# TensorE signals its edge products, turned rows and layer results by a drain behind the group

## The chip, the cores and the metric

The kernel runs on one core of a Trainium2 chip. The metric is the time of one execution on the device in microseconds (us), as the median of several runs; lower is better.

## What is computed

A graph network over 3,125 nodes with 256 features and 53,125 edges, sorted by their target. In the reference, cut to its two layers:

```
# layer 0
neighbor = segment_sum(weight[:, None] * x[src], dst)
out = (x @ W1.T + b1) + (neighbor + neighbor * x) @ W2.T + b2
out = where(out >= 0, out, 0.2 * out);  out = out / max(norm(out), 1e-12)
x = layernorm(x + out)
# layer 1: self loops added, whose edge attributes are zero
e = relu(edge_attr @ ee_w1 + ee_b1) @ ee_w2 + ee_b2
agg = segment_sum(x[src] + e, dst)
h = (1 + eps) * x + agg
h = relu(ln(h @ w1 + b1, g1, be1))      # 256 -> 1024
h = relu(ln(h @ w2 + b2, g2, be2))      # 1024 -> 1024
out = relu(ln(x + h @ w3 + b3, bn_g, bn_b))
x = layernorm(x + out)
```

## The kernel before

Nodes are worked in 25 blocks of 128 rows, edges in tiles of 128: 17 tiles per block, 8 in the last, taken in pairs (nine steps per block, the ninth a single tile; four in the last block). The program has two stages, one after the other on every engine, and each has a general version that does not run on this graph.

**The edge stage.** For each tile GpSimd (POOL) gathers 128 rows of x by the edges' sources (L970). TensorE (PE) multiplies the edge attributes by ee_w1 (`edge_layer`, L1108) for a pair of tiles into one of three banks `ps_e` and signals `edge_net`. ScalarE (ACT) and VectorE (DVE) make the message `msg` of the pair out of both, as a high part and a low remainder (L1658 and L1661 on ACT, L2162 and L2168 on DVE), and DVE signals `message`. PE sums a tile's messages per target by a product with a one-hot matrix, once for the high part (L1113) and once for the low part (L1115). The edge product runs three pairs ahead (`LEAD`) of the sums, and waits for the message of the pair two before it. When a block is summed, PE turns its four pieces of 128 columns (`turn`, L1143) and signals `s_turned`; ACT copies the turned rows to `sT`, and three small products (L1183, L1190, L1209), spread over the next blocks, give the layer's rows, which go to HBM as a table.

**The network stage.** POOL gathers rows of that table (L1031), PE sums them per target (`near_step` of the second stage, L1330 and L1335), and the block's h passes through the three layers. Here each product is made of three in `three` (L1386): high by high, high by low, low by high. Per block PE has `turn_h` (two turns of h, signals `h_turned`), `layer1` for each half of the 1,024 columns (6 products of 512 wide each, signals `z_done[0]`), `layer2` for each half (24 products each, signals `z_done[1]`), `layer3` (24 products of 256 wide in two halves, signals `y_done` after the second) and `turn_z` for each of layers 1 and 2 and each half (four turns of `zn`, L1455, signals `turned2`). Between them DVE takes statistics of the layer's rows (L2480), ACT and DVE normalize to `zn` (L1876, L2505), ACT applies scale, shift and relu to the turned rows (L1888), and DVE splits the result into high and low parts (L2523, L2525), which PE's next layer waits for.

The order on PE is written out by hand. `iteration`, which a loop runs for 21 blocks (L1584), interleaves neighbouring blocks: layer 2 of block i - 1 (first half), `turn_h` of i, the second half of layer 2, three sum tiles of i + 1, layer 1 of i, `turn_z` of layer 2 of i - 1 (both halves), further sum tiles, `turn_z` of layer 1 of i, and layer 3 of i - 1 around its second half. Each wait is either attached to the instruction behind it or stands as a semaphore instruction of PE's sequencer ahead of it.

In all these groups the last matmul carries the signal, by `mm.then_inc(...)`.

Of the kernel before, what the change touches and what calls it, by code (L numbers as in the profile page):

```python
# [31 lines left out]
N, E, D, ED, H = 3125, 53125, 256, 64, 1024  # L32
P = 128
# [22 lines left out]
KD = D // 128  # L56
KH = H // 128
# [6 lines left out]
def wait(eng, sem, value):  # L64

    if isinstance(value, int) and value <= 0:
        return
    eng.wait_ge(sem, value)
# [168 lines left out]
def exists(b):  # L237

    return not isinstance(b, int) or 0 <= b < BLOCKS
# [32 lines left out]
def gnn_program(nc, x, xT, src, dst, weight, attrT, w1T, w2T, bias01, bias02, eps_in, ee_w1, ee_b1row, ee_b1,  # L272
# [6 lines left out]
    with ExitStack() as keep:  # L279
        def sb(name, shape, dt, ctx=keep):  # L280
            return ctx.enter_context(nc.sbuf_tensor(name, shape, dt))

        def psum(name, shape, ctx):
            return ctx.enter_context(nc.psum_tensor(name, shape, F32))
# [10 lines left out]
        ident = sb("ident", [P, P], F32)  # L295
# [13 lines left out]
        with ExitStack() as ca:  # L309
            def sa(name, shape, dt):  # L310
                return sb(name, shape, dt, ca)

            def ma(name):
                return sem(name)
# [8 lines left out]
            attr = sa("attr", [ED + 1, TILES * P], F32)  # L323
# [28 lines left out]
            we1 = sa("we1", [ED + 1, D], F32)  # L352
# [13 lines left out]
            s_r = sa("s_r", [P, 2 * D], F32)  # L366
# [15 lines left out]
            ps_e = [psum(f"ps_e{n}", [P, 512], ca) for n in range(3)]  # L382
            ps_t = psum("ps_t", [128, 512], ca)
# [20 lines left out]
            edge_net = ma("edge_net")  # L404
# [6 lines left out]
            s_turned = ma("s_turned")  # L411
# [104 lines left out]
        with ExitStack() as cb:  # L516
            def s2(name, shape, dt):
                return sb(name, shape, dt, cb)

            def m2(name):  # L520
                return sem(name)
# [9 lines left out]
            w1_low = s2("w1_low", [128, KD, H], F32R)  # L531
            w2_low = s2("w2_low", [128, KH, H], F32R)
            w3_low = s2("w3_low", [128, KH, D], F32R)
            w1_high = s2("w1_high", [128, KD, H], F32R)
# [5 lines left out]
            h = s2("h", [P, D], F32)  # L540
            ident_r = s2("ident_r", [P, P], F32R)
            place(msg_base)
            w2_high = s2("w2_high", [128, KH, H], F32R)
            place(msg_base + 8 * 16 * D)
            grow = s2("grow", [P, TILES, 2 * D], F32R)
            hT = s2("hT", [128, 2, KD * P], F32R)
# [13 lines left out]
            w3_high = s2("w3_high", [128, KH, D], F32R)  # L560
# [4 lines left out]
            zn = s2("zn", [P, H], F32)  # L565
# [4 lines left out]
            ps_z = [psum(f"ps_z{n}", [P, 2, 512], cb) for n in range(2)]  # L570
            ps_tr = psum("ps_tr", [128, 2, 512], cb)
            ps_y = psum("ps_y", [P, 512], cb)
# [19 lines left out]
            h_turned = m2("h_turned")  # L592
            hT_high, hT_ready = m2("hT_high"), m2("hT_ready")
            z_done = [m2(f"z_done{n}") for n in range(2)]
# [4 lines left out]
            turned2 = [m2(f"turned2_{n}") for n in range(2)]  # L599
            relu_out = [m2(f"relu_out{n}") for n in range(2)]  # L600
            a_ready = [m2(f"a_ready{n}") for n in range(2)]
            y_done = m2("y_done")
# [56 lines left out]
            def a_of(layer, p):  # L659

                if isinstance(p, int) and (layer, p) in ((0, LAST), (1, LAST - 1)):
                    return (a2, a1)[layer]
                return (a1, a2)[layer]

            def z_of(layer, p):

                return ps_z[0] if layer == 1 and isinstance(p, int) and p == LAST else ps_z[layer]
# [424 lines left out]
        def _(pe):  # L1092
# [9 lines left out]
            def edge_layer(q, k, start=0):  # L1102

                j0, m = PAIRS[k]
                pe.wait_ge(attr_in[k // 3], 16 * (q + 1 + (1 if start else 0)))
                wait(pe, message, start + NP * q + k - 2)
                for j in range(j0, j0 + m):
                    mm = pe.matmul(ps_e[k % 3][:, (j - j0) * D:(j - j0 + 1) * D],  # L1108
                                   attr[:, j * P:(j + 1) * P], we1[:, :], start=True, stop=True)
                mm.then_inc(edge_net, 1)  # L1110

            def add_tile(bank, j, slot, start, stop):
                pe.matmul(ps_sum[bank][:, :], oh[:, slot, :], msg[:, j, 0, :], start=start, stop=False,  # L1113
# [24 lines left out]
            def turn(b):  # L1138

                pe.wait_ge(s_ready, b + 1)  # L1140
                wait(pe, sT_ready, b)
                for n in range(4):
                    mm = pe.transpose(ps_t[:, n * P:(n + 1) * P], s_r[:, n * 128:(n + 1) * 128], ident[:, :])  # L1143
                mm.then_inc(s_turned, 1)

            def count(acc, first, end, n, chain):

# [143 lines left out]
            def second_stage():  # L1291
# [83 lines left out]
                def turn_h(path, b):  # L1375
                    pe.wait_ge(h_ready, b + 1)

                    wait(pe, relu_out[0 if path.skewed else 1], 2 * b)
                    for k in range(KD):
                        mm = pe.transpose(ps_tr[:, 0, k * P:(k + 1) * P], h[:, k * 128:(k + 1) * 128], ident[:, :])  # L1380
                    mm.then_inc(h_turned, 1)

                def three(acc, left, right, stop):

                    for a, b in ((0, 0), (0, 1), (1, 0)):
                        mm = pe.matmul(acc, left[a], right[b], start=False, stop=stop and a == 1,  # L1386
                                       skip_group_check=True)
                    return mm

                def layer1(b, n):  # L1390
                    if n == 0:
                        pe.wait_ge(hT_ready, b + 1)
                    pe.wait_ge(z_open[0][n], b + 1)
                    cols = slice(n * 512, (n + 1) * 512)
                    for k in range(KD):
                        mm = three(ps_z[0][:, n, :], [hT[:, a, k * P:(k + 1) * P] for a in range(2)],
                                   [w[:, k, cols] for w in (w1_high, w1_low)], k == KD - 1)
                    mm.then_inc(z_done[0], 1)

                def layer2(b, n, first=0, end=KH):  # L1400
                    if first == 0:
                        pe.wait_ge(z_open[1][n], b + 1)
                    cols = slice(n * 512, (n + 1) * 512)
                    for k in range(first, end):
                        if n == 0 and k % 4 == 0:
                            pe.wait_ge(a_ready[0], 2 * b + k // 4 + 1)
                        mm = three(z_of(1, b)[:, n, :], [a_of(0, b)[:, a, k, :] for a in range(2)],
                                   [w[:, k, cols] for w in (w2_high, w2_low)], k == KH - 1)
                    if end == KH:
                        mm.then_inc(z_done[1], 1)  # L1410

                def layer2_with(b, n, w, first, end):

# [17 lines left out]
                def layer3(b, half):  # L1431
                    if half == 0:
                        pe.wait_ge(y_open, b + 1)
                    pe.wait_ge(a_ready[1], 2 * b + half + 1)
                    for k in range(half * KH // 2, (half + 1) * KH // 2):
                        mm = three(ps_y[:, 0:D], [a_of(1, b)[:, a, k, :] for a in range(2)],
                                   [w[:, k, :] for w in (w3_high, w3_low)], k == KH - 1)
                    if half == 1:
                        mm.then_inc(y_done, 1)

                def turn_z(path, layer, b, half, free=None):

                    if free:
                        pe.wait_ge(relu_out[free[0]], 2 * free[1] + half + 1)
                    elif layer == 0:
                        pe.wait_ge(hT_ready, b + 1)
                        wait(pe, relu_out[1], 2 * (b - 1) + half + 1)
                    else:
                        pe.wait_ge(relu_out[0], 2 * b + half + 1)
                        if path.skewed and exists(b + 1):  # L1450
                            pe.wait_ge(hT_ready, b + 2)
                    pe.wait_ge(zn_ready[layer][half], b + 1)
                    for c in range(4):
                        k = 4 * half + c
                        mm = pe.transpose(ps_tr[:, half, c * P:(c + 1) * P], zn[:, k * 128:(k + 1) * 128],  # L1455
                                          ident[:, :])
                    mm.then_inc(turned2[layer], 1)

                def is_late(i):

# [7 lines left out]
                def first_block(path):  # L1468
# [6 lines left out]
                    pe.wait_ge(dd_end[-1], DD)  # L1475
                    copy_highs(2, 4)
                    turn_h(path, 0)
                    copy_highs(4, 6)
                    pe.wait_ge(w_ready, LAYER_1 - 1)
                    layer1(0, 0)  # L1480
                    copy_highs(6, 7)
                    pe.wait_ge(w_ready, LAYER_1)
                    layer1(0, 1)
                    copy_highs(7, 9)
                    for c in path.ahead[0:2]:
                        near_step(path, 1, c)
                    turn_z(path, 0, 0, 0)
                    pe.wait_ge(w_ready, 6)
                    turn_z(path, 0, 0, 1)
                    copy_highs(9, 11)  # L1490
                    for c in path.ahead[2:]:
# [1335 lines left out]
```

## Time and profile before

| | before |
|---|---|
| time, median of 3 runs | 1,134.37 us (1,134.0 to 1,136.73) |
| span of the profiled execution | 1,477.5 us |
| PE matmul busy | 1,201.4 us (81%), 5,297 matmuls |
| DVE busy | 976.8 us (66%) |
| POOL busy | 812.9 us (55%) |
| ACT busy | 686.1 us (46%) |
| mean granted TensorE clock | 0.891 of full speed |

The profiled execution is 343 us longer than the timed median. Its durations of single instructions can be read as they are; its idle stretches can't be carried over to a timed run as they are. The profile records the start of every matmul and models its end, so that rows of neighbouring matmuls overlap. "PEld" is the load of the weights that a matmul uses, and an engine's name with a q behind it is its sequencer, which works through waits, register work and drains.

### The profile page before, as it was taken

The numbers are of one execution on the slowest core, as the hardware profiler recorded it, in microseconds if no ns is written. First come the engines' busy times: TensorE is split into PE (matmuls) and PEld (weight loads), VectorE is DVE, ScalarE is ACT, GpSimd is POOL, SyncE is SP. The second block draws the span as 40 slices with busy tenths as digits, with TensorE's granted clock in tenths as the row PEclk, the third lists the DMA queues.
The fourth block names the chain that finished last, engine by engine and source line by source line (L and its number), as shares of the span: only waits on it lengthen the run. The fifth ranks groups of instructions, "written<-read, shape, count | busy, mean of one in ns | idle before, by whom it ended". The sixth has DMA issues, their size and how long they took to land.

```text
span 1477.5 us, 21215 instructions
## 1 busy us (share of the span) xinstructions
PE 1201.4 (81%) x5297; PEld 977.9 (66%) x5297; DVE 976.8 (66%) x2795; ACT 686.1 (46%) x1677; POOL 812.9 (55%) x840
## 2 busy tenths in 40 slices
PE   4788877787777887778777889888898898898897
PEld 3576666566666665566555677677776777776676
DVE  4767755667656775667666666666666676676575
ACT  2455644556445554455453443443533443443444
POOL 7555555455554555545645565566565566566530
PEclk9798887888878888788878899999999999999999
DMA  6345544445444444435565555656665566566540
GB/s 202 105 120 145 151 130 144 125 142 147 134 143 128 128 127 119 126 114 148 146 203 163 165 169 172 185 167 183 176 185 166 174 176 178 171 185 180 161 119 13
DMA packets 106088, 222.13 MB, mean 150 GB/s; under 512 B 20003, under 2 KB 57369, under 8 KB 106010
## 3 DMA queue, kind: packets, MB, share of 16 engines
q0 software_dynamic: 53408, 164.16, 39.1%
q1 hardware_dynamic: 52602, 57.11, 12.4%
q8 instruction: 27, 0.44, 0.1%
q14 instruction: 51, 0.42, 0.1%
HBM read 203.96 MB, written 17.23 MB: 150 GB/s over the span
## 4 chain that ended last, share of the span: by engine, by line
PE 34%; another core or an unknown queue 21%; DVE 16%; issue 16%; ACT 11%; DVEq 1%; DMA 1%; POOL 1%; ACTq 0%; POOLq 0%
PE ps_z L1386 8%; PE ps_e L1108 7%; PE ps_sum L1115 3%; PE ps_sum L1113 3%; ACT msg L1658 3%; ACT aF L1888 3%; PE ps_y L1386 3%; PE ps_s L1330 3%; DVE msg L2162 2%; DVE oh L216 2%; PE ps_tr L1455 2%; DVE msg L2168 2%; PE ps_w L1209 2%; ACT msg L1661 2%
## 5 line engine op out<-in xcount | busy, mean ns | idle before, releaser
L970 POOL DMA_INDIRECT raw<-in_x,src_all x399 | 385.6, 966 | 321.9 <-DVE msg L2168 177.2
L1031 POOL DMA_INDIRECT grow<-table_dram,src_all x401 | 392.7, 979 | 275.0 <-issue 115.1
L1108 PE MATMUL ps_e<-we,attr 65*128 65x256 f32 x832 | 251.1, 427 | 150.7 <-DVE msg L2168 127.0
L2162 DVE SCALAR_TENSOR_TENSOR msg<-raw,w_sb,msg 128x256 fp32r<-128x256 f32 x416 | 183.0, 478 | 242.5 <-issue 130.5
L1108 PEld LDWEIGHTS ps_e<-we,attr 65*128 65x128 f32 x832 | 171.5, 214 | 200.4 <-issue 173.3
L1661 ACT ACTIVATE msg<-ps_e 128x512 fp32r<-128x512 f32 (+1 forms) x220 | 124.3, 565 | 310.2 <-remote 221.1
L1113 PE MATMUL ps_sum<-msg,oh 128*128 128x512 f32 x464 | 255.8, 551 | 9.2 <-DVE msg L2168 8.8
L1386 PE MATMUL ps_z<-w_high,a 128*128 128x512 f32 x784 | 255.5, 395 | 7.7 <-issue 6.3
L216 DVE TENSOR_SCALAR oh<-lane,rel 128x128 fp32r<-128x128 f32 x871 | 208.1, 297 | 18.9 <-issue 15.7
L1115 PE MATMUL ps_sum<-msg,oh 128*128 128x512 f32 x464 | 210.1, 453 | 0.0
L1658 ACT ACTIVATE msg<-raw,w_sb 128x256 fp32r<-128x256 f32 x416 | 188.1, 498 | 10.3 <-issue 7.7
L1386 PEld LDWEIGHTS ps_z<-w_high,a 128*128 128x128 f32 x784 | 147.0, 188 | 40.1 <-issue 9.5
L1888 ACT ACTIVATE aF<-ps_tr,be,g 128x128 f32<-128x128 f32 x392 | 147.3, 464 | 53.7 <-PE ps_tr L1455 33.1
L1386 PE MATMUL ps_z<-w_low,a 128*128 128x512 f32 x392 | 153.4, 391 | 1.0 <-issue 0.8
L2168 DVE SCALAR_TENSOR_TENSOR msg<-ps_e,msg 128x512 fp32r<-128x512 f32 (+1 forms) x220 | 143.6, 653 | 0.0
L1455 PE MATMUL ps_tr<-ident,zn 128*128 128x128 f32 x400 | 64.3, 301 | 76.5 <-issue 38.8
L1113 PEld LDWEIGHTS ps_sum<-msg,oh 128*128 128x128 f32 x464 | 102.9, 222 | 34.0 <-issue 11.7
L1115 PEld LDWEIGHTS ps_sum<-msg,oh 128*128 128x128 f32 x464 | 104.1, 224 | 22.4
L1455 PEld LDWEIGHTS ps_tr<-ident,zn 128*128 128x128 f32 x400 | 50.1, 155 | 89.0 <-issue 88.4
L1330 PE MATMUL ps_s<-grow,oh 128*128 128x512 f32 x365 | 104.2, 429 | 0.4 <-issue 0.4
L1386 PE MATMUL ps_y<-w_high,a 128*128 128x256 f32 x400 | 89.6, 306 | 4.1 <-DVE a L2538 2.1
L1386 PEld LDWEIGHTS ps_z<-w_low,a 128*128 128x128 f32 x392 | 73.8, 188 | 18.6 <-issue 5.2
(189 smaller groups left out, 1591.6 us busy)
## 6 DMA issues: line engine op xcount, KB each, us to landing
attr<-in_attrT SPq DMA_DIRECT2D x50, 192.0 KB
raw<-in_x,src_all POOLq DMA_INDIRECT x416
grow<-table_dram,src_all POOLq DMA_INDIRECT x401
w_raw<-in_m_w SPq DMA_DIRECT2D x48, 128.0 KB
table_dram<-table SPq DMA_DIRECT2D x23, 256.0 KB
attr<-in_attrT SPq DMA_DIRECT2D x24, 160.0 KB
xs<-in_x SPq DMA_DIRECT2D x24, 128.0 KB
xTb<-in_xT SPq DMA_DIRECT2D x24, 128.0 KB
```

The lines of the kernel that those rows point to most:

```text
L216: ins = dve.tensor_scalar(out_[:, i, :], lanes, which[:, i:i + 1], None, ALU.is_equal)
L970: pool.indirect_dma_start(out=raw[:, j, :], out_offset=None, in_=x, in_offset=bass.IndirectOffsetOnAxis(ap=src_all[:, q * TILES + j:q * TI ...
L1031: pool.indirect_dma_start(out=grow[:, j, :].bitcast(F32), out_offset=None, in_=table_dram, in_offset=bass.IndirectOffsetOnAxis(ap=src_all[ ...
L1108: mm = pe.matmul(ps_e[k % 3][:, (j - j0) * D:(j - j0 + 1) * D], attr[:, j * P:(j + 1) * P], we1[:, :], start=True, stop=True)
L1113: pe.matmul(ps_sum[bank][:, :], oh[:, slot, :], msg[:, j, 0, :], start=start, stop=False, skip_group_check=True)
L1115: return pe.matmul(ps_sum[bank][:, :], oh[:, slot, :], msg[:, j, 1, :], start=False, stop=stop, skip_group_check=True)
L1386: mm = pe.matmul(acc, left[a], right[b], start=False, stop=stop and a == 1, skip_group_check=True)
L1658: act.activation(msg[:, j, 0, 0:D], raw[:, j, :], ACT.Copy, scale=w_sb[:, tile_cols(n, j)])
L1661: act.activation(msg[:, j0:j0 + m, 0, D:2 * D], ps_e[k % 3][:, 0:m * D].rearrange("p (j d) -> p j d", d=D), ACT.Relu).then_inc(high, 1)
L1888: ins = act.activation(aF[layer][:, k, :], ps_tr[:, half, c * P:(c + 1) * P], ACT.Relu, bias=bb[:, k:k + 1], scale=gg[:, k:k + 1])
L2162: dve.scalar_tensor_tensor(msg[:, j, 1, 0:D], raw[:, j, :], w_sb[:, tile_cols(n, j)], msg[:, j, 0, 0:D].bitcast(F32), ALU.mult, ALU.subtract)
L2168: dve.scalar_tensor_tensor(msg[:, j0:j0 + m, 1, D:2 * D], ps_e[k % 3][:, 0:m * D].rearrange("p (j d) -> p j d", d=D), 0.0, msg[:, j0:j0 + ...
```

## The change

On PE, in `edge_layer`, `turn`, `turn_h`, `layer1`, `layer2`, `layer3` and `turn_z`, the signal is taken off the group's last matmul. Behind the group stands a drain, and that carries the signal. The semaphores, their values and all who wait for them stay as they are, and so does the order of all other instructions on every engine. The signals of the sum tiles (`summed`, `sum_done`), of the small products (`dense`, `edge_dense`), of layer 2 of block 0 (which has its own code, `layer2_with`) and of layer 3 of the last block stay on matmuls.

```diff
@@ edge_layer
-                    mm = pe.matmul(ps_e[k % 3][:, (j - j0) * D:(j - j0 + 1) * D],
-                                   attr[:, j * P:(j + 1) * P], we1[:, :], start=True, stop=True)
-                mm.then_inc(edge_net, 1)
+                    pe.matmul(ps_e[k % 3][:, (j - j0) * D:(j - j0 + 1) * D],
+                              attr[:, j * P:(j + 1) * P], we1[:, :], start=True, stop=True)
+                pe.drain().then_inc(edge_net, 1)
@@ turn
-                mm.then_inc(s_turned, 1)
+                pe.drain().then_inc(s_turned, 1)
@@ turn_h
-                    mm.then_inc(h_turned, 1)
+                    pe.drain().then_inc(h_turned, 1)
@@ layer1
-                    mm.then_inc(z_done[0], 1)
+                    pe.drain().then_inc(z_done[0], 1)
@@ layer2
                     if end == KH:
-                        mm.then_inc(z_done[1], 1)
+                        pe.drain().then_inc(z_done[1], 1)
@@ layer3
                     if half == 1:
-                        mm.then_inc(y_done, 1)
+                        pe.drain().then_inc(y_done, 1)
@@ turn_z
-                    mm.then_inc(turned2[layer], 1)
+                    pe.drain().then_inc(turned2[layer], 1)
```

## Rows read from the trace of the kernel before

**Rows 1.** Windows: length, busy of PE, PEld, DVE, ACT, POOL; clock, DMA share, GB/s:

```profile
0.00:25.30 25.30, 14.11 (x36) 10.30 (x37) 13.94 (x40) 7.81 (x16) 18.12 (x23) 1.00 0.84 248
25.30:731.50 706.20, 553.19 (x2133) 443.23 (x2132) 467.16 (x1367) 367.05 (x890) 384.62 (x398) 0.83 0.46 132
...
731.50:769.60 38.10, 26.41 (x110) 20.07 (x109) 22.64 (x64) 18.29 (x44) 17.57 (x19) 0.80 0.60 178
...
769.60:1424.10 654.50, 565.27 (x2785) 468.27 (x2785) 439.31 (x1244) 266.95 (x665) 391.70 (x400) 0.95 0.60 175
```

**Rows 2.** Who waited on PE for whom: total us, times, longest; edge, then network stage:

```profile
PE ps_e L1108 <- DVE msg L2168: 127.0, 37, 7.6
...
PE ps_tr L1455 <- issue: 38.8, 21, 4.5
PE ps_tr L1455 <- ACT zn L1876: 35.0, 16, 6.0
```

**Rows 3.** Grouped instructions: count | busy us, mean ns | idle before us:

```profile
L1386 PE MATMUL ps_z<-w_high,a 128*128 128x512 f32 x784 | 255.5, 395 | 7.7 <-issue 6.3 <-DVE a L2525 1.2
L1108 PE MATMUL ps_e<-we,attr 65*128 65x256 f32 x832 | 251.1, 427 | 150.7 <-DVE msg L2168 127.0 <-issue 18.8 <-remote 4.9
```

**Rows 4.** Timeline of an edge group and its sum tiles: start us, us, matmuls, then loads:

```profile
606.10 1.03 PE L1108 MATMUL ps_e<-we,attr 65*128 65x256 f32 x4
606.78 0.59 PE L1113 MATMUL ps_sum<-msg,oh 128*128 128x512 f32 x1
...
606.75 0.19 PEld L1113 LDWEIGHTS ps_sum<-msg,oh 128*128 128x128 f32 x1
```

**Rows 5.** Timeline of PE at turn_z and layer 3, network stage:

```profile
1126.08 0.60 PE L1455 MATMUL ps_tr<-ident,zn 128*128 128x128 f32 x4
...
1127.47 0.40 PE L1386 MATMUL ps_y<-w_high,a 128*128 128x256 f32 x2
...
1127.83 0.28 PE L1386 MATMUL ps_y<-w_high,a 128*128 128x256 f32 x1
...
1126.40 0.19 PEld L1386 LDWEIGHTS ps_y<-w_high,a 128*128 128x128 f32 x1
```

**Rows 6.** Timeline behind layer 2, then the wait of L1393 (last: its time):

```profile
1110.19 0.39 PE L1386 MATMUL ps_z<-w_high,a 128*128 128x512 f32 x1
1110.42 0.84 PE L1330 MATMUL ps_s<-grow,oh 128*128 128x512 f32 x3
...
1111.52 0.40 PE L1386 MATMUL ps_z<-w_low,hT 128*128 128x512 f32 x1
...
1110.19 0.64 PEld L1330 LDWEIGHTS ps_s<-grow,oh 128*128 128x128 f32 x3
1111.18 0.19 PEld L1386 LDWEIGHTS ps_z<-w_high,hT 128*128 128x128 f32 x1 [0.34 <-DVE hT L2475]
...
L1393 PEldq EVENT_SEMAPHORE  x1: 51/51/51, 1110.1 to 1110.1; - x1
```

**Rows 7.** Timeline at the end: the last product and who takes it:

```profile
1469.90 0.28 PE L1386 MATMUL ps_y<-w_high,a 128*128 128x256 f32 x1
1470.22 0.42 DVE L2556 TENSOR_TENSOR t<-ps_y,hbx 128x256 f32<-128x256 f32 x1 [0.40 <-PE ps_y L1386]
```

**Rows 8.** PE's sequencer: duration ns min/median/max, first and last start us:

```profile
L279 PEldq DRAIN  x1: 68/68/68, 1472.6 to 1472.6; - x1
...
L1126 PEldq EVENT_SEMAPHORE  x23: 51/51/51, 81.7 to 734.1; - x23
...
L1584 PEldq COMPARE_BRANCH  x21: 76/208/228, 850.4 to 1404.2; - x21
```

**Rows 9.** Timeline of POOL, one gather (one of a row of such):

```profile
613.31 0.95 POOL L970 DMA_INDIRECT raw<-in_x,src_all  x1 [0.30 <-issue]
```

**Rows 10.** Chain of work, start us, us, what; then the window around it as Rows 1:

```profile
631.22 0.43 PE ps_sum L1113
...
631.00:633.00 2.00, 2.00 (x6) 1.61 (x5) 1.70 (x7) 2.00 (x6) 0.70 (x1) 0.50 0.58 168
```

More of the change, by code:

```diff
@@ L1142, in turn @@
                 for n in range(4):
-                    mm = pe.transpose(ps_t[:, n * P:(n + 1) * P], s_r[:, n * 128:(n + 1) * 128], ident[:, :])
-                mm.then_inc(s_turned, 1)
+                    pe.transpose(ps_t[:, n * P:(n + 1) * P], s_r[:, n * 128:(n + 1) * 128], ident[:, :])
+                pe.drain().then_inc(s_turned, 1)
             def count(acc, first, end, n, chain):
@@ L1379, in turn_h @@
                     for k in range(KD):
-                        mm = pe.transpose(ps_tr[:, 0, k * P:(k + 1) * P], h[:, k * 128:(k + 1) * 128], ident[:, :])
-                    mm.then_inc(h_turned, 1)
+                        pe.transpose(ps_tr[:, 0, k * P:(k + 1) * P], h[:, k * 128:(k + 1) * 128], ident[:, :])
+                    pe.drain().then_inc(h_turned, 1)
                 def three(acc, left, right, stop):
@@ L1395, in layer1 @@
                     for k in range(KD):
-                        mm = three(ps_z[0][:, n, :], [hT[:, a, k * P:(k + 1) * P] for a in range(2)],
-                                   [w[:, k, cols] for w in (w1_high, w1_low)], k == KD - 1)
-                    mm.then_inc(z_done[0], 1)
+                        three(ps_z[0][:, n, :], [hT[:, a, k * P:(k + 1) * P] for a in range(2)],
+                              [w[:, k, cols] for w in (w1_high, w1_low)], k == KD - 1)
+                    pe.drain().then_inc(z_done[0], 1)
                 def layer2(b, n, first=0, end=KH):
@@ L1406, in layer2 @@
                             pe.wait_ge(a_ready[0], 2 * b + k // 4 + 1)
-                        mm = three(z_of(1, b)[:, n, :], [a_of(0, b)[:, a, k, :] for a in range(2)],
-                                   [w[:, k, cols] for w in (w2_high, w2_low)], k == KH - 1)
+                        three(z_of(1, b)[:, n, :], [a_of(0, b)[:, a, k, :] for a in range(2)],
+                              [w[:, k, cols] for w in (w2_high, w2_low)], k == KH - 1)
                     if end == KH:
-                        mm.then_inc(z_done[1], 1)
+                        pe.drain().then_inc(z_done[1], 1)
                 def layer2_with(b, n, w, first, end):
@@ L1435, in layer3 @@
                     for k in range(half * KH // 2, (half + 1) * KH // 2):
-                        mm = three(ps_y[:, 0:D], [a_of(1, b)[:, a, k, :] for a in range(2)],
-                                   [w[:, k, :] for w in (w3_high, w3_low)], k == KH - 1)
+                        three(ps_y[:, 0:D], [a_of(1, b)[:, a, k, :] for a in range(2)],
+                              [w[:, k, :] for w in (w3_high, w3_low)], k == KH - 1)
                     if half == 1:
-                        mm.then_inc(y_done, 1)
+                        pe.drain().then_inc(y_done, 1)
                 def turn_z(path, layer, b, half, free=None):
@@ L1454, in turn_z @@
                         k = 4 * half + c
-                        mm = pe.transpose(ps_tr[:, half, c * P:(c + 1) * P], zn[:, k * 128:(k + 1) * 128],
-                                          ident[:, :])
-                    mm.then_inc(turned2[layer], 1)
+                        pe.transpose(ps_tr[:, half, c * P:(c + 1) * P], zn[:, k * 128:(k + 1) * 128],
+                                     ident[:, :])
+                    pe.drain().then_inc(turned2[layer], 1)
                 def is_late(i):
```

## Prediction

> **What bounds the kernel now.** I read four views in this order: the busy time of two long windows, the list of who waited for whom on TensorE, the grouped instructions, and then single instructions of two short stretches.
>
> The windows [rows 1] split the span into an edge stage (25.3 to 731.5 us) and a network stage (769.6 to 1424.1 us). TensorE (PE) is the busiest engine in both, 553 of 706 us and 565 of 655 us. Its waits [rows 2] are few in kind (the rows are the long ones). In the edge stage it waits 127 us for messages, all of it ahead of an edge product (L1108) and in only 37 places. In the network stage nearly the whole wait, 38.8 + 35.0 us, is ahead of the turn of a normalized layer (L1455), some 3 us in each of 24 blocks. Everywhere else PE runs one matmul into the next.
>
> How tight is that stream? Busy time overstates it, since each matmul row overlaps the next one. What counts is the distance from start to start. A 512-wide product follows the last after 0.225 us (three in 0.84, the last 0.39 long), a 256-wide one of the last layer after 0.12, a turn (128 wide) after 0.11, four in 0.60 [rows 5, 6]; an edge matmul after 0.217, four in 1.03, the last 0.38 long [rows 4]. With counts from the list of groups (two of some forty in [rows 3]): 1,476 of layers 1 and 2, 928 of the edge stage's sums and 365 of the network stage's, 2,769 x 0.225 = 623; 600 of layer 3 x 0.12 = 72; 832 of the edge product x 0.217 = 181; 400 turns of z x 0.11 = 44; the other 696 of all 5,297, mostly 128 and 256 wide, at an estimated 0.17 each, 118. That makes 1,038 us at the full clock, some 476 of them in the edge stage (181 + 209 and 86 of the others) and 562 in the network stage.
>
> The profiled execution took 1,477.5 us, the timed median is 1,134. That is less than PE's own 1,201 us of busy time in the profile, so the timed run cannot hold the idle stretches that the profile shows: it has 1,134 - 1,038 = 96 us of PE time that is not stream. Some 28 of these no change of this kind can use (11 idle in the first 25 and some 10 of the 12 at the change of stages, 38 us long with 26 busy [rows 1]; 7 from the last product, 1470.18 [rows 7], to the span's end). **So a timed run has at most 68 us of slack on PE, the profiled one over 200 in its waits alone.** This decides more than anything else below.
>
> **The change part by part.** Nothing is moved and no wait is added; on the path that runs, 493 groups lose the signal on their last matmul and get a drain behind it that signals. They are 220 edge groups (24 blocks of 9 pairs, the last of 4), 25 turns of sums, 25 of h, 50 of layer 1, 49 of layer 2 (the first of block 0 has its own code, untouched), 24 of layer 3 (the last block has its own), 100 turns of z.
>
> What goes: the signals on matmuls. They cost nothing today. In [rows 6] the last matmul of a layer-2 group, which signals, starts at 1110.19 and the next group at 1110.42, the same distance as inside a group.
>
> What comes: the drain is an instruction of PE's sequencer, and nothing behind it is handed to the array until it is through. Today the sequencer runs ahead: the wait of L1393 for layer 1 is done at 1110.1, when PE still has a product of layer 2 and three sum tiles to start [rows 6]. And the weight load of the next group starts with the last matmul of this one. That overlap is what a drain takes away. Three cases:
> - Edge group. Its four matmuls end at 607.13, and the weight load of the sum tile starts at 606.75 [rows 4]. With a drain the load starts after 607.13 + 0.068 (the only TensorE drain in the trace, on an idle engine) + 0.051 (the wait that follows it) [rows 8] + some 0.03 to start, at 607.28. Shift 0.53 us, x 220 = 117 us.
> - A 512-wide group: last matmul 1110.19 to 1110.58, next load today at 1110.19, with a drain at 1110.73. After a stop the next pair comes closer: load 1111.18, second matmul 1111.52, 0.34 apart, against two steps of 0.225 in the stream [rows 6]. Shift 0.54 - 0.11 = 0.43.
> - A turn: four end at 1126.68, next load today at 1126.40; with a drain 1126.83, shift 0.43 [rows 5]. Layer 3: its last matmul runs 0.28 from 1127.83 [rows 5], and the next load starts with it; 0.43 again. So (25 + 248) x 0.43 = 117 us.
> - Behind layer 3 comes the loop's end (a branch of 0.208 [rows 8] and three shorter instructions at some 0.04, 0.32 us), hidden today under products in the queue, exposed behind a drain: 21 x 0.32 = 7 us.
>
> Sum: 117 + 117 + 7 = **241 us of PE time**. Lower bound of the price: the tail of a matmul past its successor's start, 0.39 - 0.23 = 0.16, plus drain and wait 0.12, 0.28 each, 138 us in all. Upper bound: each drain is followed not by one but by two sequencer instructions, or by register work in the loop, and costs 0.13 more (0.051 of work and the pause behind it), 305 us. I take 241, since it is built from the very places.
>
> What signals lose: today a consumer starts 0.04 us after the modelled end of a product (1469.90 + 0.28, next the tensor_tensor of L2556 at 1470.22 [rows 7]). With a drain it starts about 0.1 later. On the other engines this adds some 0.1 to each link of the chain products, statistics, normalize, turn.
>
> What hides it. In the network stage the three drains between the end of layer 2 and the turn that waits for it (layer 2 itself, layer 1 twice, 1.3 us) fall into that wait of 3 us, 24 x 1.3 = 31 us, if the timed run has it. In the edge stage GpSimd starts a gather each 0.95 + 0.30 us [rows 9], so 416 of them take at least 520 us, and PE has 520 - 476 = 44 us free; that leaves some 24 of the 68 for the network stage. A stream with breaks in it never fills all of that: I count 20 in each stage as used. **1,134 + 241 - 40 = 1,335 us.**
>
> Against the profiled execution the same sum gives less, since it holds more idle time: the edge stage's 128 us half hidden in its 152 us of waits, +64; the network stage 113 - 31, +82; so 1,477.5 + 146, near 1,625.
>
> A rule on the other side of the row: the Trainium skill, "VectorE: DVE Perf Modes", section "The DRAIN you can't avoid", tells of boilerplate drains of a constant 12 ns on all five engines. By it the 493 would be 6 us. The trace disagrees even for an idle PE, 68 ns [rows 8]. "PSUM — Partial Sum Buffer", section "Engine vs sequencer instructions", says that a drain waits for the engine to go fully idle; by that rule the price is the one worked out above, and no row of this trace has a drain behind running products to show it.
>
> **Rivals.**
> (1) *The gathers pace the edge stage, and a drain overlaps more than I think.* With all 44 us used there and the lower price: 245 x 0.28 - 44 = 25, and 248 x 0.28 + 7 - 20 = 56 in the network stage, 1,134 + 81 = 1,215; with 0.43 everywhere it is 1,289. For it: PE waits 127 us for messages in the edge stage [rows 2], and these come from gathers. Against it: nothing shows a weight load that starts ahead of a drain.
> (2) *Dearer.* Upper price, 305 - 40: 1,399. Or the clock: in the edge stage the granted clock averages 0.83 of 2.4 GHz [rows 1], and in a stretch at 0.50, the level of 1.2 GHz, in which PE had gone idle, a 512-wide product takes 0.43 us of the chain [rows 10]. More gaps may cost more of it; a further tenth of the stream at that level would be 1,038 x 0.1 x (0.43 - 0.225) / 0.225 = 95 us, less what vanished long waits give back. 1,370 to 1,430.
> (3) *The other side: no loss.* The drain returns when all is handed to the array, not when it is through, and the sequencer's lead covers it: 493 x (0.068 + 0.051) = 59 us of sequencer time off the path. Then 1,134, within 0.3% of before. It decides if the sequencer's lead behind a group is over 0.12 us, which [rows 6] show it is; but then consumers would read unfinished sums, which a drain is there to prevent. A gain would need signals that come earlier, and there are 0.04 us to win at each at most.
>
> **How the numbers follow.** My forecast (1,290 to 1,370) 0.57; rival 1 (1,215 to 1,289) 0.22; rival 2 0.17; rival 3 0.03; a gain 0.01. The range 1,230 to 1,410 leaves out the foot of rival 1, rival 3 and the top of rival 2, some 0.15 together. About 0.3% is what a measurement can tell from no change: faster 0.01, same 0.03, slower 0.96.
>
> **What the profile after would show.** Each price: the weight load of L1113 behind an edge group starting 0.1 to 0.2 us after that group's last matmul has ended, instead of with it; gaps of this kind, put down to nothing the profile shows, some 490 times; drains with a row each whose time grows with what is in flight. The stream: fewer waits of PE for messages and for zn. Wrong if weight loads still start under a drained group's last matmul (rival 3), if that start comes less than 0.1 us behind it, while PE still has waits for messages (rival 1), or if the clock of either window falls by over 0.05 (rival 2). The forecast falls too if the timed cost per drain, the difference over 493, lies outside 0.3 to 0.5 us.

## The result, and the profile after

| | before | after |
|---|---|---|
| time, median | 1,134.35 us | 1,320.49 us (1,320.31 to 1,335.18) |
| ratio | | 1.1661, 95% interval 1.1606 to 1.1716 |
| span of the profiled execution | 1,477.5 us | 1,318.7 us |
| the same, second profile of before | 1,135.1 us | |
| PE matmul busy (second profile) | 1,081.8 us (95%) | 1,174.4 us (89%) |
| idle of PE, span less busy (same) | 53 us | 144 us |

The change costs 186 us, 16.6%. The kernel before, unchanged and profiled again (first experiment below), has a span of 1,135.1 us, close to its timed median, so all traces of after are compared with that second one. Ratios leave out disturbed executions, which only experiment 8 had: three of its six, at 1,447.42 to 1,457.88 us.

The page of after: the span, the busy time of each engine with its share, the granted TensorE clock in forty slices, and the chain of work that ended last.

```profile
span 1318.7 us, 21708 instructions
...
PE 1174.4 (89%) x5297; PEld 877.7 (67%) x5297; DVE 985.8 (75%) x2795; ACT 691.0 (52%) x1677; POOL 810.7 (61%) x840
...
PEclk9999999999999999999999999999999999999999
...
PEld 50%; issue 27%; PEldq 12%; DVE 7%; DMA 2%; PE 1%; ACT 1%; POOL 0%; POOLq 0%; DVEq 0%; ACTq 0%
```

The same lines of the second profile of before:

```profile
span 1135.1 us, 21215 instructions
...
PE 1081.8 (95%) x5297; PEld 894.6 (79%) x5297; DVE 986.4 (87%) x2795; ACT 688.1 (61%) x1677; POOL 803.3 (71%) x840
...
PE 50%; POOL 21%; issue 17%; DVE 7%; DMA 3%; ACT 1%; POOLq 0%; DVEq 0%; ACTq 0%
```

There are 493 instructions more, the drains, and the same number of matmuls. PE's busy time is 93 us longer all the same, and that is no further work: a matmul's row overlaps the next one's, and where the stream breaks the overlap is gone, so that the union of the rows grows. Busy and idle time together give the 184 us by which the spans differ. The chain is what changed. Before, it ran over matmuls (PE 50%) and over gathers (POOL 21%). After, it runs over weight loads (PEld 50%), over time in which PE waited for nothing that the profile shows (issue 27%) and over the drains (PEldq 12%), and POOL is no longer in it: a weight load that starts late, behind a drain, is what the end waits for.

An edge group in the timeline of after (start us, length us, in brackets the idle time before and its releaser), which answers to [rows 4], and then the drains of L1110 that touch this stretch (count, shortest/median/longest ns, first and last start):

```profile
300.83 1.03 PE L1108 MATMUL ps_e<-we,attr 65*128 65x256 f32 x4
...
301.92 0.60 ACT L1661 ACTIVATE msg<-ps_e 128x512 fp32r<-128x512 f32 x1 [1.52 <-PEq L1110]
302.06 0.19 PEld L1113 LDWEIGHTS ps_sum<-msg,oh 128*128 128x128 f32 x1 [0.60 <-issue]
302.09 0.47 PE L1113 MATMUL ps_sum<-msg,oh 128*128 128x512 f32 x1 [0.23 <-issue]
...
302.40 0.39 PE L1115 MATMUL ps_sum<-msg,oh 128*128 128x512 f32 x1
```

```profile
L1110 PEldq DRAIN  x2: 2335/2338/2342, 299.5 to 302.2; - x2
```

The edge matmuls' modelled end is 301.86. The first drain runs from 299.5 for 2.34 us and ends at about 301.9 (its row gives starts in tenths; by the trace it ends 0.02 us behind the matmuls); ACT, which waits for it, starts at 301.92. The next weight load starts at 302.06, 0.20 behind the matmuls' end, where before the change it started under them. The same place in the second profile of before:

```profile
302.44 1.03 PE L1108 MATMUL ps_e<-we,attr 65*128 65x256 f32 x4
303.12 0.59 PE L1113 MATMUL ps_sum<-msg,oh 128*128 128x512 f32 x1
303.55 0.39 PE L1115 MATMUL ps_sum<-msg,oh 128*128 128x512 f32 x1
```

The last of the four edge matmuls starts 0.65 behind the first. From it to the second matmul behind the group are 303.55 - 303.09 = 0.46 us before and 302.40 - 301.48 = 0.92 after. Read in this way, to the second matmul, which takes in that the next two matmuls stand closer together after a stop, the typical price of each kind of group is:

| group | drains | shift each, us | sum, us |
|---|---|---|---|
| edge product | 220 | 0.467 | 102.7 |
| turn of the sums | 25 | 0.464 | 11.6 |
| turn of h | 25 | 0.343 | 8.6 |
| layer 1 | 50 | 0.347, 0.424 | 19.3 |
| layer 2 | 49 | 0.523, 0.580 | 27.1 |
| turn of z | 100 | 0.343 to 0.565, mean 0.473 | 47.3 |
| layer 3 | 24 | 0.945 at the loop's end (21), 0.43 taken for the other 3 | 21.1 |
| all | 493 | mean 0.48 | 238 |

Behind layer 3 stands the loop's end, and there the stop is the longest:

```profile
912.34 0.28 PE L1386 MATMUL ps_y<-w_high,a 128*128 128x256 f32 x1
913.30 0.49 PE L1386 MATMUL ps_z<-w_high,a 128*128 128x512 f32 x1 [0.69 <-issue]
913.63 0.40 PE L1386 MATMUL ps_z<-w_low,a 128*128 128x512 f32 x1
```

From 912.34 to 913.63 are 1.29 us, against 0.345 in a stream (0.12 + 0.225).

**By stage.** The edge stage ends with the last sum matmul (L1115); its rows before and after (count, shortest/median/longest ns, first and last start us):

```profile
L1115 PE MATMUL ps_sum<-msg,oh x464: 387/395/628, 21.1 to 533.4; 128*128 128x512 f32 x155
```

```profile
L1115 PE MATMUL ps_sum<-msg,oh x464: 387/392/628, 21.9 to 606.5; 128*128 128x512 f32 x155
```

So the edge stage grew by 73.1 us, the network stage by (1,318.7 - 606.5) - (1,135.1 - 533.4) = 110.5. Of the 114.3 us of drains in the first, 41 are hidden; of the 123.4 in the second, 13.

Both traces hold the same 5,297 matmuls in the same order, so the growth can also be added up place by place, from start to start. At the drained places the spacing grew by 112 us in the edge stage and by 118 in the network stage, 230 in all where the table of typical prices has 238. All other spacings shrank, by 39 us and by 8. In the edge stage 30 of those 39 us lie ahead of an edge product or of the first product of a tile's sum, the places where PE had to wait for messages before the change; now it comes late enough not to. In the network stage, then, some 5 of the 13 hidden us are the table's, and 8 are left; two executions that have no drain in this stage differ there by up to 3 us.

The windows of each stage, after and then before (start and end, length; busy of PE, PEld, DVE, ACT, POOL; clock, DMA share, GB/s), which answer to [rows 1]:

```profile
25.00:606.00 581.00, 524.25 (x2182) 380.39 (x2180) 483.49 (x1385) 378.46 (x907) 398.60 (x408) 1.00 0.59 165
635.00:1300.00 665.00, 602.63 (x2919) 463.18 (x2918) 449.90 (x1263) 275.99 (x695) 377.94 (x392) 1.00 0.58 169
```

```profile
25.00:533.00 508.00, 486.86 (x2180) 390.11 (x2179) 482.65 (x1384) 374.67 (x907) 384.63 (x406) 1.00 0.67 187
561.00:1115.00 554.00, 547.69 (x2909) 468.08 (x2908) 449.75 (x1263) 275.84 (x694) 382.51 (x394) 0.99 0.70 204
```

The clock is at its upper level, 2.4 GHz, in all four. PE's idle share went from 4% to 10% in the edge stage and from 1% to 9% in the network stage.

**Who waits now.** On PE the wait for messages of [rows 2] is gone, and time put down to nothing ("issue") stands first (total us, times, longest):

```profile
PE ps_sum L1113 <- issue: 39.1, 167, 0.4
PE ps_z L1386 <- issue: 15.4, 25, 0.7
...
PE ps_tr L1455 <- ACT zn L1876: 0.9, 1, 0.9
PE ps_e L1108 <- DVE msg L2168: 0.9, 3, 0.4
```

The other engines wait for drains:

```profile
ACT msg L1661 <- PEq L1110: 149.0, 134, 2.5
...
ACT aF L1888 <- PEq L1457: 98.7, 69, 2.2
...
POOL raw L970 <- PEq L1144: 62.0, 21, 6.1
```

These last three look like the loss and are not, as the fourth experiment shows: these engines now follow PE.

### The profile page after: what moved, and what is told of

It reads as the page before. It is cut to its first block, busy times and chain, and to the rows that moved or that the text cites. A ratio compares the mean times of both kernels' runs of the same rounds, so it can differ in the third digit from the quotient of the medians.

```text
span 1318.7 us, 21708 instructions
## 1 busy us (share of the span) xinstructions
PE 1174.4 (89%) x5297; PEld 877.7 (67%) x5297; DVE 985.8 (75%) x2795; ACT 691.0 (52%) x1677; POOL 810.7 (61%) x840
## 4 chain that ended last, share of the span: by engine, by line
PEld 50%; issue 27%; PEldq 12%; DVE 7%; DMA 2%; PE 1%; ACT 1%; POOL 0%; POOLq 0%; DVEq 0%; ACTq 0%
PEld ps_z L1386 19%; PEld ps_e L1108 9%; PEld ps_y L1386 5%; PEld ps_sum L1115 5%; PEldq L1110 3%; PEldq L1144 3%; PEld ps_tr L1455 3%; PEld ps_s L1330 3%; PEld ps_sum L1113 3%; DMA raw<-in_x,src_all 2%; DVE msg L2162 2%; DVE oh L216 1%; DVE msg L2168 1%; PEld ps_d L1190 1%; PEld ps_w L1209 1%
## 5 line engine op out<-in xcount | busy, mean ns | idle before, releaser
L1031 POOL DMA_INDIRECT grow<-table_dram,src_all x401 | 386.5, 964 | 257.7 <-issue 112.1
L1113 PE MATMUL ps_sum<-msg,oh 128*128 128x512 f32 x464 | 199.7, 430 | 51.3 <-issue 39.1
L1108 PE MATMUL ps_e<-we,attr 65*128 65x256 f32 x832 | 222.9, 388 | 7.4 <-issue 5.3
L1108 PEld LDWEIGHTS ps_e<-we,attr 65*128 65x128 f32 x832 | 157.8, 193 | 40.3 <-issue 14.6
L1115 PE MATMUL ps_sum<-msg,oh 128*128 128x512 f32 x464 | 183.1, 395 | 0.0
L1113 PEld LDWEIGHTS ps_sum<-msg,oh 128*128 128x128 f32 x464 | 87.3, 188 | 143.0 <-issue 102.4
L2480 DVE BATCH_NORM_STATS2 bs<-ps_z 128x6 f32<-128x512 f32 x100 | 69.6, 698 | 69.7 <-PEq L1410 41.0
L1330 PE MATMUL ps_s<-grow,oh 128*128 128x512 f32 x365 | 96.5, 403 | 15.2 <-issue 15.1
L2523 DVE CAST a<-aF 128x512 fp32r<-128x512 f32 x98 | 42.0, 429 | 71.4 <-ACT aF L1888 71.4
L1115 PEld LDWEIGHTS ps_sum<-msg,oh 128*128 128x128 f32 x464 | 87.9, 189 | 10.6
L1330 PEld LDWEIGHTS ps_s<-grow,oh 128*128 128x128 f32 x365 | 64.8, 188 | 41.6 <-issue 29.6
L1899 ACT ACTIVATE fm<-fm,ln_eps 128x1 f32<-128x1 f32 x50 | 14.7, 295 | 137.1 <-DVE fm L2485 137.1
```

The lines of the kernel that those rows point to most:

```text
L1031: pool.indirect_dma_start(out=grow[:, j, :].bitcast(F32), out_offset=None, in_=table_dram, in_offset=bass.IndirectOffsetOnAxis(ap=src_all[ ...
L1108: pe.matmul(ps_e[k % 3][:, (j - j0) * D:(j - j0 + 1) * D], attr[:, j * P:(j + 1) * P], we1[:, :], start=True, stop=True)
L1115: return pe.matmul(ps_sum[bank][:, :], oh[:, slot, :], msg[:, j, 1, :], start=False, stop=stop, skip_group_check=True)
L1330: return pe.matmul(ps_s[:, :], oh[:, slot, :], grow[:, j, :], start=start, stop=stop, skip_group_check=True)
```

## The experiments

**1. The kernel before, once more.** No edit. The question was whether the long waits of the first profile belong to the kernel.

> The kernel before, unchanged, for a second profiled execution. The change's profile has a span of 1,318.7 us beside a timed median of 1,320.5, at a mean clock of 0.998; the one of before has 1,477.5 beside 1,134, at 0.891. Theory A: the first profile of before was one disturbed execution; a second one has a span within 1% of 1,134 and a clock near 1. Theory B: the program before is slowed by being profiled, whenever it is (its sequencers run ahead and are held by the records); the span is again near 1,478 with 5 to 7 us pauses of ScalarE and VectorE in each block of the edge stage.

Measured: 1,136.94 us (one execution; seven others of the same kernel beside it have a median of 1,135.65), span 1,135.1 us, mean clock 0.993. The waits of PE that answer to [rows 2]:

```profile
PE ps_e L1108 <- DVE msg L2168: 12.8, 22, 3.1
...
PE ps_tr L1455 <- ACT zn L1876: 3.5, 3, 1.4
```

127 us of waiting for messages are 12.8, and the 74 us ahead of the turn of z are 3.5 and 0.7. So the first profile's 343 us are no fixed property of the program, nor of profiling it as such. What disturbed that execution is not known.

**2. The two halves of the change.** One kernel has the drains of the edge products alone (220), the other the remaining 273. Against the change, e1 puts back, at all places but the first, the form of before:

```diff
-                pe.drain().then_inc(s_turned, 1)
+                mm.then_inc(s_turned, 1)
```

and e2 does so in `edge_layer` only:

```diff
-                pe.drain().then_inc(edge_net, 1)
+                mm.then_inc(edge_net, 1)
```

> Drains behind the 220 edge groups alone, all other groups as before. Stream theory: from the second matmul behind the group, the change's trace shows 0.47 us lost at each, 103 us in all; with the 44 us of slack that I estimated for the edge stage, of which 20 used, 1,134 + 103 - 20 = 1,217; with all 44 used 1,193. Rival, late signals: the loss comes from consumers that start later, and the edge signal is the one that ScalarE waits for 134 times; then this part carries most of the 186 us, over 1,280.

> Drains behind the turns and the layers (273 groups), the edge groups as before. Stream theory: the trace of the change shows 134 us lost at these places (0.34 to 0.58 each, 0.94 behind layer 3); 20 hidden, 1,134 + 134 - 20 = 1,248. With the edges-only kernel it adds up to the change, since the stages follow one another: the two losses sum to 186 within 10. Rival, late signals: under 1,200 if the edge signal carries the loss.

Measured: the edges alone 1,196.82 us, ratio 1.0575 (1.0502 to 1.0648), +61. The others alone 1,248.16 us, 1.0992 (1.0973 to 1.1010), +112.5. Together 174, and the change lost 186. The last sum matmul of e1 and of e2:

```profile
L1115 PE MATMUL ps_sum<-msg,oh x464: 387/395/628, 22.0 to 594.9; 128*128 128x512 f32 x155
```

```profile
L1115 PE MATMUL ps_sum<-msg,oh x464: 387/395/628, 21.4 to 533.5; 128*128 128x512 f32 x155
```

With the 25 drains of the sums' turn alone in this stage, the edge stage ends when it did before (533.5 against 533.4): their 11.6 us are hidden. Beside the edges' drains they are not (594.9 to 606.5, 11.6 us). That is the missing 12 us between 174 and 186: the cover of the edge stage is one sum, and it was used up already.

**3. How large is the cover?** Drains behind every third edge product (74) and every second one (98, those of odd k), signals on matmuls elsewhere:

```diff
-                pe.drain().then_inc(edge_net, 1)
+                if k % 2:
+                    pe.drain().then_inc(edge_net, 1)
+                else:
+                    mm.then_inc(edge_net, 1)
```

(in the other, `if k % 3 == 0:`)

> Drains behind every third edge group alone (pairs 0, 3 and 6 of a block, 74 groups), else as before. At 0.47 us each they take 35 us of TensorE. Slack theory: the edge stage is paced by GpSimd's gathers and hid 42 of the 103 us of 220 drains, so these 35 are hidden whole: within 5 us of before. Rival, proportional: each edge drain costs 61 / 220 = 0.28 us whatever their number, +21 us.

> Drains behind every second edge group alone (pairs 1, 3, 5, 7, 98 groups). At 0.47 us each 46 us. Slack theory: 42 hidden, +4 us, up to +12 if the places are uneven. Rival, proportional: +27 us.

Measured: 74 drains 1,136.67 us, ratio 1.0005 (0.9994 to 1.0015), nothing. 98 drains 1,143.35 us, 1.0070 (1.0047 to 1.0092), +7.6. At 0.467 each the 98 are 46 us, so 38 are hidden; the 220 of e1 are 103 and lost 61, so 42 are hidden. The loss is a bent line: nothing at 35 us of drains, 7.6 us at 46, and from there nearly one for one (from 98 to 220 drains, 57 us of them, 53.5 us of loss).

What makes the cover is, by the traces, the row of gathers. In the second profile of before, 372 of the 399 wait for nothing but their own issue, 0.3 us each at most:

```profile
POOL raw L970 <- issue: 113.3, 372, 0.3
```

Their first and last start, in that profile and in e8 (ns, first and last start us):

```profile
L970 POOL DMA_INDIRECT raw<-in_x,src_all x399: 942/946/1222, 25.8 to 524.5; - x200
```

```profile
L970 POOL DMA_INDIRECT raw<-in_x,src_all x399: 942/946/1233, 25.2 to 525.5; - x200
```

399 of them in 499 us are 1.25 us each, [rows 9]'s 0.95 + 0.30, and 74 breaks in PE's stream leave that as it is. In after the last starts at 592.9, and POOL waits 62.0 us for the drain of L1144 (above), in e1 53.7 us for the turn itself: now PE sets the pace. No run changed the pace of the gathers themselves.

**4. Is it the late signal or the stopped stream?** The signal goes back to the matmul, and a drain that signals nothing stands behind every one of the 493 groups (shown against the change):

```diff
-                pe.drain().then_inc(edge_net, 1)
+                mm.then_inc(edge_net, 1)
+                pe.drain()
```

> All 493 drains stand, but the signal stays on the group's last matmul, so that consumers are told as early as before. Stream theory: within 1% of the change (1,307 to 1,334), since what costs is that nothing behind the drain is handed to the array. Rival, late signals: the drain row shows the signal 0.02 us behind the matmul's modelled end, and if the lateness carries the loss this kernel is back near 1,134, or at least under 1,250.

Measured: 1,316.22 us, ratio 1.1632 (1.1557 to 1.1708). 182 of the 186 us are there with early signals. Of the change's waits, ACT's for an edge product is almost as long:

```profile
ACT msg L1668 <- PE ps_e L1108: 143.1, 134, 2.3
```

So the stream carries 182 us. What is left for the lateness of the signals is 4 us, which is less than the two intervals overlap.

**5. Any instruction, or a drain?** As e3, with a no-operation of PE's sequencer in the drain's place:

```diff
-                pe.drain().then_inc(edge_net, 1)
+                mm.then_inc(edge_net, 1)
+                pe.nop(nofuse=True)
```

> No drain: signals on the matmuls as before, and behind each of the 493 groups a no-op of the sequencer, which waits for nothing. Run-ahead theory: one more instruction is hidden by the sequencer's lead, within 5 us of before. Rival, the sequencer's time counts: 493 x 0.12 = 59 us more than before.

Measured: 1,136.32 us, ratio 1.0002 (0.9992 to 1.0012), the time of before. But it isn't shown that the no-operations ran. The page of this run counts as many instructions as that of before, where each variant with drains counts its drains on top:

```profile
span 1132.0 us, 21215 instructions
```

No row of its trace is a no-operation, and between the wait ahead of an edge group and the wait behind it the sequencer leaves 74 ns, as before. So whether another instruction of the sequencer would be free at these places stays open. That the price is in the drain's wait and not in having one instruction more rests on the next experiment.

**6. Two drains behind each group,** the second with the signal, against the change:

```diff
+                pe.drain()
                 pe.drain().then_inc(edge_net, 1)
```

> Behind each of the 493 groups two drains, the second one signals. What a drain costs is the emptied array or the instruction itself. Emptied array: the second finds an idle engine and costs its own time and the pause behind it, some 0.12 us, 493 x 0.12 = 59 us more than the change, about 1,380. Rival, a fixed price per drain instruction: another 230 us, about 1,550.

Measured: 1,356.35 us, ratio 1.1981 (1.1928 to 1.2035), 35.9 over the change or 0.073 for each second drain. First and second drain of the edge groups in the trace (count, shortest/median/longest ns, first and last start):

```profile
L1110 PEldq DRAIN  x220: 1068/1902/4420, 10.3 to 615.0; - x110
...
L1111 PEldq DRAIN  x220: 13/13/134, 12.5 to 616.7; - x110
```

The first stands for 1.9 us because the sequencer reaches it that long before PE's queue is empty, the second for 13 ns. Behind an edge group the next weight load starts 0.20 us after the last matmul's end with one drain and 0.27 with two. A drain that finds PE emptied thus costs some 0.07 us of the path. If the first has the same fixed part, the remaining 0.27 to 0.5 us of its price is the overlap that it takes away.

**7. Layer 3 alone, layer 1 alone.** e9 keeps only the 24 drains behind layer 3, e10 only the 50 behind layer 1. The first asks for the price at the loop's end, the second whether the wait for zn hides anything. Each kernel is the kernel before with one group's signal moved, in e9:

```diff
-                        mm.then_inc(y_done, 1)
+                        pe.drain().then_inc(y_done, 1)
```

> Drains behind layer 3 alone (24 groups, 22 of which stand ahead of the loop's end). The change's trace shows 0.94 us lost there each, since add, branch, move and register work of the loop's end come to light too: 21 to 23 us more than before, less some 2 to 4 that waits in the network stage take. Rival, the drain alone costs (0.47 each): 11 us more.

> Drains behind the halves of layer 1 alone (50 groups). The second profile of before shows next to no wait of TensorE for zn (3.5 us in all), unlike the first, from which I took 3 us in each block. Stream theory with that trace: 25 x 0.35 + 25 x 0.42 = 19 us, shown nearly whole, +15 to +19. Rival, the wait for zn hides them, as the prediction had it: +0 to +5.

Measured: layer 3 1,155.90 us, ratio 1.0180 (1.0161 to 1.0199), +20.6 where the table above has 21.1: nearly nothing is hidden, and the price of 0.945 at the loop's end holds. Layer 1 1,152.69 us, 1.0146 (1.0128 to 1.0165), +17.4 of 19.3: nearly nothing is hidden either, though layer 1's drains stand just ahead of the turn of layer 2's zn.

**8. A drain behind every step of sums of the edge stage too,** 243 more on top of the change, without a signal of their own, at the end of `near_step`:

```diff
                 mm.then_inc(summed, near_inc(b, c))
+                pe.drain()
```

> The change, and a further drain behind each of the sum steps of the edge stage (some 240; their signals stay on the matmuls). The change's edge stage is no longer paced by gathers, so nothing is left to hide them: 240 x 0.47 = 113 us more than the change, 1,420 to 1,440. Rival, the chain from gather to message also has slack in it that takes part: under 1,390.

Measured: 1,428.15 us (1,425.66 to 1,431.40), ratio 1.2561 (1.2531 to 1.2591), 108 us over the change. The trace has the further drains in one row:

```profile
L1137 PEldq DRAIN  x243: 592/1188/3778, 21.4 to 739.2; - x122
```

That is 0.443 us for each, close to the 0.467 of an edge group: with no cover left a drain shows nearly its full price.

## Why the prediction was right

1,335 us were predicted and 1,320.49 measured, inside the range of 1,230 to 1,410. Step by step:

- **The slack of a timed run.** That the timed run could not hold the idle stretches of the profiled one was right and decided the rest. The second profile of before has 53 us of idle time on PE in all, where the first has 276. Had the cover been taken from the first profile's 200 us of waits, the forecast would have been 1,134 + 241 - 200 = 1,175 us.
- **The cost, 241 us.** The table above has 238 (230 place by place). That the sum came so close is in part luck, for its terms err in both directions: 14 us too much for the edge products, 11 too little for the other 273 groups. The edge product was put at 0.53 and is 0.467: the prediction took off, behind a layer, the 0.11 by which the next pair comes closer, and left that out behind an edge group. At the place shown above the weight load comes 0.58 us later (302.06 against 301.48, the last edge matmul's start), and the pair then stands 0.12 closer (0.31 against 0.43). Layer 3 with the loop's end was put at 0.75 and is 0.945; the loop's end adds some 0.5 and not 0.32, and which of its instructions takes the rest was not tried. Layer 2 (0.43 for 0.523 and 0.580) and the turns of z (0.43 for 0.473) are dearer, because two sequencer instructions or register work stand behind the drain: the next weight load comes 0.05 us after a drain if nothing stands between, 0.18 if one sequencer instruction does, 0.28 if two do (medians by the trace of after; 0.075, 0.20 and 0.30 behind the last matmul's end). That was the prediction's upper price, and about a fifth of the groups have it (layer 2 and half of the turns of z).
- **What hides it, 40 us.** 52 are hidden by the table (238 - 186), 47 place by place. The edge stage's slack was worked out right, 44 us from the row of gathers, and only 20 of it was taken as usable, on the ground that a stream with breaks in it never fills all of its slack. That ground is wrong here: 38 of 46 us were hidden in e7 and 34 of 35 in e8. The edge product runs three pairs ahead of the sums, which may be why a small delay anywhere does no harm as long as the total of delays stays under the slack; that was not tried apart. This is the term that was mis-sized by most: 21 us too little here, 7 too much in the network stage, and 3 too much in the sum, 17 together, against the 14.5 by which the forecast was high (the spans differ by 184 us, the medians by 186). With all 44 us taken in the edge stage, as the rival sum had it, the forecast would have been 1,311.
- **The network stage's cover was the wrong mechanism.** Three drains per block were to fall into a wait of 3 us for zn. That wait is a property of the disturbed execution; the second profile has 3.5 us of it in all, and e10 lost 17.4 of its 19.3 us. What is hidden in this stage is 13 us by the table against 20 forecast, and 8 when the matmuls' spacings are added up place by place: 3 at three turns of z that stand behind sum tiles, 2 ahead of the window products (L1335), the rest in small pieces. So the 20 us taken here had no ground, and that they were small kept the forecast near.
- **The profiled execution, near 1,625 us.** Wrong by 306: its base of 1,477.5 was the disturbed execution's.
- **Late signals.** Some 0.1 per link of the chain was said and not priced; e3 against the change leaves 4 us for all of it.
- **Rival 1** (gathers pace, cheap drains) had the right place. Its 44 us in the edge stage are what is hidden, 41 to 42, but its lower price of 0.28 is below every typical price in the table (0.343 at least). No weight load starts under a drained group. It starts 0.20 us behind the group's end at an edge group, and 0.07 where nothing stands behind the drain; that is less than the 0.1 us named as this rival's sign, but PE has next to no wait for messages left with it, and the price is 0.343 even there.
- **Rival 2** asked for a falling clock. It did not fall: 1.00 in both windows of after, 1.00 and 0.99 before. The first profile's 0.83 and 0.95 were its own.
- **Rival 3** (no loss) fell with the drain rows: the drain stands until the last matmul's modelled end, 1.9 us at the median behind an edge group (e5), and the sequencer's lead is spent in it. The timed cost per drain, 186 us over 493, is 0.38 us, inside the 0.3 to 0.5 that the forecast asked for.
- **Two rules.** The Trainium skill, "PSUM — Partial Sum Buffer", section "Engine vs sequencer instructions", says that a drain waits until the engine is fully idle. The trace agrees: the drain of the edge group above ends at about 301.9, the modelled end of its last matmul is 301.86. The Trainium skill's "VectorE: DVE Perf Modes", section "The DRAIN you can't avoid", gives some 12 ns for a boilerplate drain on any engine. The prediction held the 68 ns of [rows 8] against it and called that the only TensorE drain of the trace. It is not; another stands at the program's start, in the first profile of before:

```profile
L2819 PEldq DRAIN  x1: 8/8/8, 0.3 to 0.3; - x1
```

So the two boilerplate drains of PE have 8 and 68 ns. A second drain behind a first has a row of 13 ns, so the figure fits the row of a drain that finds PE just emptied; the path still pays 73 ns for it, and for a drain with products in flight it is no guide.

## What to carry to other kernels

A signal on a group's last matmul costs nothing that shows here; a drain behind the group, whether it carries the signal or not, costs 0.34 to 0.58 us of the matmul stream here, and 0.95 where a loop's end follows, because the next weight load no longer starts under the last matmul. Such breaks cost nothing while another engine paces the stage, up to that stage's slack as one sum over all breaks, and nearly one for one beyond it: work out the slack from the pacing engine's start-to-start distance times its count. And when a profiled execution is clearly longer than the timed median, as by 30% here, no wait in it is to be used as cover before a second profile shows it too.

## What the runs showed of the hardware

- A second drain right behind a first has a row of 13 ns and costs 73 ns of time; the drains at the program's start and end have 8 and 68 ns.
- A sequencer instruction behind a drain runs after it, not ahead: from the drain's end to the next weight load are 0.05 us with nothing between, 0.18 with one such instruction, 0.28 with two. The drain itself ends 0.02 us behind the last matmul's modelled end.
- A drain with a loop's end behind it takes 0.945 us from PE's stream, about 0.5 more than a drain elsewhere.
